# Layer 2's state-space scan laid out as 8 channels x 16 states per tile, and its routing counts in two matmuls

## The reference

```python
xc = silu(conv1d(xi, 4 taps) + conv_b)             # xi, z = split(xn @ W_in), 256 channels each
dt_lo, Bm, Cm = split(xc @ W_xp, [8, 24])          # 8, 16 and 16 columns
delta = softplus(dt_lo @ W_dt + dt_bias)           # 256 channels
def step(h, (dt_t, B_t, C_t, u_t)):                # h: 256 channels x 16 states
    h = h * exp(dt_t[..., None] * A) + (dt_t * u_t)[..., None] * B_t[:, None, :]
    return h, einsum('bdn,bn->bd', h, C_t)
y = (scan(step) + xc * D_skip) * silu(z);  s = y @ W_out + x
# feed-forward: probs = softmax(x @ Wr + br); two best of 16 banks; relu(x W1 + b1) W2 + b2, weighted
```

## Time and profile before

| | |
|---|---|
| median of 3 runs | 4643.89 us (4642.11 to 4647.07) |
| the profiled execution: its time, its span | 4658.04 us, 4656.4 us |
| granted PE clock, mean of the span | 0.793 |
| layer2_route | about 1150 to 1347 us of the span |
| layer2_mix | 1347 to about 2350 us; first scan at 1391.9, last at 2332.0 |

### The profile page before, as it was taken

How to read it: one execution, slowest core, us unless ns; L and a number is a source line. 1 busy time by engine, 2 the same in 40 slices (tenths; PEclk the granted TensorE clock), 3 DMA queues, 4 the chain that set the end, 5 groups by cost and what they waited for, 6 DMA issues and landing times. The chain is left out here.

```text
span 4656.4 us, 50785 instructions
## 1 busy us (share of the span) xinstructions
PE 3423.9 (74%) x17802; PEld 1842.6 (40%) x17802; DVE 2642.8 (57%) x3696; ACT 1828.2 (39%) x3692; POOL 1538.3 (33%) x1231
## 2 busy tenths in 40 slices
PE   5888888883538788788757677676776857778587
PEld 3444444441424344344323334333343334343343
DVE  3444444442547777777655566555665656556565
ACT  3333333331214444444424434344343434434344
POOL 0000000003316665656644253332533424334242
PEclk8888888885557777777768879688797988959789
DMA  1000000002212222222100000000000000000000
GB/s 80 7 7 7 7 7 7 7 5 74 72 42 63 67 67 67 67 67 59 59 16 5 8 1 5 8 5 8 1 5 8 5 8 1 8 6 5 8 1 8
DMA packets 70704, 111.46 MB, mean 24 GB/s; under 512 B 8640, under 2 KB 46016, under 8 KB 69952
## 3 DMA queue, kind: packets, MB, share of 16 engines
q1 hardware_dynamic: 65088, 97.47, 6.5%
q0 software_dynamic: 5376, 11.02, 0.9%
HBM read 81.71 MB, written 26.74 MB: 23 GB/s over the span
## 5 line engine op out<-in xcount | busy, mean ns | idle before, releaser
L369 ACT ACTIVATE l_PT<-PB 128x512 f32<-128x512 f32 x512 | 277.9, 594 | 539.1 <-PE PB L280 539.1
L280 PE MATMUL PB<-l_QM,l_KP 32*128 32x256 f32 x2048 | 375.2, 497 | 131.6 <-DVE l_QM L418 75.9
L407 DVE TENSOR_REDUCE keep_MXP<-PB 128x4 f32<-128x1024 f32 x256 | 301.5, 1220 | 106.8 <-PE PB L253 106.8
L280 PEld LDWEIGHTS PB<-l_QM,l_KP 32*128 32x128 f32 x2048 | 241.3, 243 | 256.4 <-ACT l_PT L369 99.9
L1308 DVE TENSOR_TENSOR_SCAN l_ST<-l_DA,l_DB 128x1024 f32<-128x1024 f32 x128 | 313.7, 2451 | 42.0 <-ACT l_DA L1196 32.8
L1355 POOL TENSOR_TENSOR l_CA<-l_ST,l_CN 128x512 f32<-128x512 f32 x128 | 182.6, 1426 | 397.6 <-DVE l_ST L1308 346.0
L703 POOL MEMSET l_KV<- 128x4 f32 x8 | 0.8, 105 | 918.5 <-POOLq L109 918.5
L1515 POOL TENSOR_TENSOR l_PT<-l_PT,l_PEN 128x512 f32<-128x512 f32 x168 | 212.5, 1284 | 184.5 <-ACT l_PT L369 184.5
L1089 PE MATMUL PB<-l_CA,consts 128*128 128x512 f32 x256 | 199.2, 872 | 71.4 <-POOL l_CA L1355 71.4
L1779 POOL TENSOR_TENSOR l3f_SQ<-l3f_RW 128x512 f32<-128x512 f32 x128 | 146.8, 1147 | 302.4 <-ACT l3f_RW L1645 302.4
L1302 DVE TENSOR_TENSOR l_DB<-l_DU,PB 128x1024 f32<-128x1024 f32 x128 | 155.4, 1214 | 154.1 <-PE PB L1079 153.4
(11 more groups left out here) (416 smaller groups left out, 7934.3 us busy)
## 6 DMA issues: line engine op xcount, KB each, us to landing
l_WB<-in_w2f_dram SPq DMA_DIRECT2D x80, 578.0 KB, 3.4
l_XR<-xs_mid SPq DMA_DIRECT2D x80, 64.0 KB, 3.5
ys_mid<-l_YO SPq DMA_DIRECT2D x80, 64.0 KB, 3.3
w3fs<-in_w3f_dram SPq DMA_DIRECT2D x1, 3125.0 KB, 16.6
keep_XI<-in_x_dram SPq DMA_DIRECT2D x9, 256.0 KB, 3.0
x_mid<-keep_X SPq DMA_DIRECT2D x9, 256.0 KB, 3.0
s_mid<-keep_S SPq DMA_DIRECT2D x9, 256.0 KB, 2.0
keep_SI<-s_mid SPq DMA_DIRECT2D x9, 256.0 KB, 2.6
```

The costliest lines, as they stand in the source:

```text
L280: last = nc.tensor.matmul(PB[:, 4 + u % STBANKS, kt * SEQ:(kt + 1) * SEQ], b.KP[rows, a, i, k0:k0 + 128], b.QM[rows, n % 2, :], start=True ...
L369: nc.scalar.activation(b.PT[:, u % PSLOTS].rearrange("p k q -> p (k q)"), PB[:, 4 + u % STBANKS, :], ACT.Exp).then_inc(s.exp_done, 1)
L407: nc.vector.tensor_reduce(dst[:, 2 * pair:2 * pair + 2, :, 16 + n % 2], PB[:, 2 * pair:2 * pair + 2, :].rearrange("p r (t k) -> p r t k", ...
```

## The change

In the mix, a turn now handles 16 channels instead of one state: partition p of a tile is channel p // 16 of a group of 8 and state p % 16, and the tile has two such groups of 512 tokens. There are still 16 turns a chunk (`PAIRS`).

- B and C depend on the state and the token alone: they are spread once per chunk (head steps 12 and 13, two matmuls with `statesel`, copied by ACT to `BT` and `CT`). `CN` goes.
- delta and delta*x must now be spread from 8 channels to 128 partitions in every turn: `spread_pairs` issues four matmuls of K = 32 (`rowsel`), two from `DL` for the next turn into banks 0 and 1, two from `DU` for this turn into banks 2 and 3. For one turn they lie in the four row strips of the array. ACT `decay` reads banks 0 and 1, DVE `drive` banks 2 and 3.
- POOL multiplies ST by C in place, one instruction of 2 x 512; PE sums over states with ones matrices of 32 columns (`add_states`, four matmuls in the four column strips every second turn, bank 4). Sums are taken by DVE (`take_sums`) twice a chunk.
- The head uses one bank (7) instead of two, one matmul at a time. ACT takes over the copies of xi and z and the bias add of delta; z goes through a copy and one silu of 1024 columns; x_proj is two matmuls instead of four. POOL takes over DU = delta*x (`drives`, turn 13).
- The expert tile uses bank 5 for rows, hidden and the final projection, 6 for out; tiles run in turns 5 to 14 (`FIRST` = 5).
- ST gets four buffers instead of two. Three constants are added (696 columns).
- In the routing stage `counts` is two matmuls of 64 columns, ahead of `ln_tensor` on PE; `place` makes the running base with four small adds and stands behind `ln_vector` on DVE.

```diff
 # layer2_route
-                    for t in range(TT):
-                        o = PB[:, 6, t * E2:(t + 1) * E2]
-                        nc.tensor.matmul(o, c.before, b.OC[:, t, :], start=True, stop=t == 0)
-                        for u in range(t):
-                            nc.tensor.matmul(o, c.ones, b.OC[:, u, :], start=False, stop=u == t - 1)
...
+                    nc.tensor.matmul(PB[:, 6, 0:TT * E2], c.before, each, start=True, stop=True)
+                    nc.tensor.matmul(PB[:, 6, TT * E2:2 * TT * E2], c.ones, each, start=True, stop=True).then_inc(s.count_ready, 1)
...
 # layer2_mix, PE
+                def spread(bank, src, k, n, e):
+                    h, i, strip = place(n)          # n // 8, n % 8 // 2, 2 * (n % 2)
+                    q = 32 * (strip + e)
+                    return nc.tensor.matmul(PB[:, bank + e, :], c.rowsel[q:q + 32, i * 128:(i + 1) * 128],
+                                            src[q:q + 32, k % 2, h, :], start=True, stop=True)
+
+                def spread_pairs(k, n):
+                    g = PAIRS * k + n
+                    ahead = g + 1 < PAIRS * CHUNKS
+                    k1, n1 = divmod(g + 1, PAIRS)
+                    if ahead:
+                        pe.wait_ge(s.decay_ready, g + 1)
+                        if n1 == 0:
+                            pe.wait_ge(s.delta_ready, k1 + 1)
...
+                    if g:
+                        pe.wait_ge(s.drive_done, g)
+                    for e in range(2):
+                        if ahead:
+                            spread(0, b.DL, k1, n1, e).then_inc(s.delta_spread, 1)
+                        spread(PAIR0, b.DU, k, n, e).then_inc(s.drive_spread, 1)
...
+                def add_states(k, q):
+                    h, i, _ = place(2 * q)
+                    pe.wait_ge(s.part_ready, PAIRS * k + 2 * q + 2)
...
+                    for n in (2 * q, 2 * q + 1):
+                        for e in range(2):
+                            strip = 2 * (n % 2) + e
+                            last = nc.tensor.matmul(PB[32 * strip:32 * strip + 32, SUMS, :], c.states[:, 24 - 8 * i:56 - 8 * i], b.ST[:, (PAIRS * k + n) % RING, e, :],
+                                                    start=i == 0, stop=i == 3, tile_position=(0, 32 * strip))
...
 # layer2_mix, ACT
+                    for e in range(2):
+                        act.wait_ge(s.delta_spread, 2 * g + e + 1)
+                        group = 16 * h + 4 * (strip + e) + i
+                        last = nc.scalar.activation(b.DA[:, g % 2, e, :].rearrange("p (s t) -> p s t", t=SEQ)[:, :, 1:SEQ],
+                                                    PB[:, e, :].rearrange("p (s t) -> p s t", t=SEQ)[:, :, 1:SEQ],
+                                                    ACT.Exp, scale=c.aneg[:, group:group + 1])
                     last.then_inc(s.decay_ready, 1)
-                    act.wait_ge(s.c_ready, g + 1)
...
-                    nc.scalar.activation(b.CN[:, g % 2, :], PB[:, 1, :], ACT.Copy).then_inc(s.c_copied, 1)
...
 # layer2_mix, DVE
+                    dve.wait_ge(s.drive_spread, 2 * g + 2)
+                    nc.vector.tensor_tensor(b.DB[:, g % 2], PB[:, PAIR0:PAIR0 + 2, :], b.BT[:, k % 2, :].unsqueeze(1).broadcast_to([128, 2, T]),
+                                            ALU.mult).then_inc(s.drive_done, 1)
...
 # layer2_mix, POOL
+                        nc.gpsimd.tensor_tensor(b.ST[:, g % RING], b.ST[:, g % RING], b.CT[:, k % 2, :].unsqueeze(1).broadcast_to([128, 2, T]),
+                                                ALU.mult).then_inc(s.part_ready, 1)
+                        if n == 13 and k + 1 < CHUNKS:
+                            drives(k + 1)
```

More of the change, by code:

```diff
@@ L56 @@
           ("dist", 2 * SEQ), ("qcos", SEQ), ("qsin", SEQ), ("kcos", SEQ), ("ksin", SEQ), ("rot", 128),
[L57 removed]
+          ("window", 4 * 128), ("expert", E2), ("states", 56), ("statesel", 128), ("rowsel", 512), ("tile", TILES), ("full", TOKENS // 128), ("eps", 1), ("one", 1), ("aeps", 1), ("pow", 1), ("lnnorm", 1)]
 W0 = [("q", NA * 128), ("k", NA * 128), ("v", 128), ("out", NA * 128), ("w2", 1024), ("win", 128), ("w1c", 8),
@@ L1057, in head @@
                     elif step == 9:
-                        pe.wait_ge(s.silu_z, 2 * k + 2)
+                        pe.wait_ge(s.z_copied, 2 * k + 2)
                         pe.wait_ge(s.silu_x, 2 * k + 2)
                         for h in range(2):
-                            nc.tensor.matmul(PB[0:DTR, 6, :], w.xp[:, h * 72:h * 72 + DTR], b.XC[:, p, h, :], start=h == 0, stop=h == 1)
-                        for h in range(2):
-                            last = nc.tensor.matmul(PB[0:64, 7, :], w.xp[:, h * 72 + DTR:h * 72 + 72], b.XC[:, p, h, :], start=h == 0, stop=h == 1)
+                            last = nc.tensor.matmul(PB[0:96, LANE, :], w.xp[:, h * 96:(h + 1) * 96], b.XC[:, p, h, :], start=h == 0, stop=h == 1)
@@ L1092, in project @@
                 def project(k):
                     pe.wait_ge(s.y_gated, k + 1)
-                    pe.wait_ge(s.rows_taken, SLOTS * (k + 1))
+                    pe.wait_ge(s.hid_done, 4 * SLOTS * (k + 1))
                     for h in range(2):
-                        last = nc.tensor.matmul(PB[:, 2, :], w.out[:, h * 128:(h + 1) * 128], b.YG[:, h, :], start=h == 0, stop=h == 1)
+                        last = nc.tensor.matmul(PB[:, WORK, :], w.out[:, h * 128:(h + 1) * 128], b.YG[:, h, :], start=h == 0, stop=h == 1)
@@ L1107, in tile_hidden @@
+                    if j % SLOTS == 0 and k:
+                        pe.wait_ge(s.s_added, k)
+                    nc.tensor.transpose(PB[:, WORK, 0:128], b.XR[:, j % 2, :], c.ident).then_inc(s.rows_ready, 1)
                 def tile_hidden(j):
@@ L1193, in decay @@
+                def decay(k, n):
+                    g = PAIRS * k + n
+                    h, i, strip = place(n)
                     if g >= 2:
                         act.wait_ge(s.state_ready, g - 1)
-                    for h in range(2):
-                        last = nc.scalar.activation(b.DA[:, g % 2, h, :].rearrange("p (s t) -> p s t", t=SEQ)[:, :, 1:SEQ],
-                                                    b.DL[:, p, h, :].rearrange("p (s t) -> p s t", t=SEQ)[:, :, 1:SEQ],
-                                                    ACT.Exp, scale=c.aneg[:, h * NS + n:h * NS + n + 1])
+                    for e in range(2):
+                        act.wait_ge(s.delta_spread, 2 * g + e + 1)
[3 more added lines that the diff above has]
+                                                    ACT.Exp, scale=c.aneg[:, group:group + 1])
```

365 lines of the change are left out of this document (182 added, 183 removed).

## The result

The changed kernel takes 4759.33 us in the median of 4 runs (4755.87 to 4785.53), the kernel before 4645.48 beside it: 1.0252 times as long, 95% interval 1.0209 to 1.0294. It is slower, by 114 us; the forecast was 4869, the range 4680 to 4980. The profiled execution took 4755.87 us with a span of 4754.3, which is 97.9 more than the span before.

What follows compares the result with a forecast made beforehand. No engine was full; expert turns were bound by the weights' load loop (6.97 us), at the low clock by PE itself. Mix +247, last chunk +11, ends +7, routing -40: +225 on 4643.9 gives 4869 us, range 4680 to 4980.

Steps and rivals of the forecast that it cites:

- The loop: Mix, expert turns: the spread waits for ACT's decay behind relus and head; bare loop 6.27 us full clock, 9.41 low.
- the two bounds: Mix: each turn's time at full and at low clock; a chunk 121 or 169 us, against 119.7 before.
- The spreads: Mix, PE: four row strips overlap, 1.05 us a turn at full clock, 2.01 low; twice the spreading costs nothing more.
- The clock: Mix: mostly low clock because PE idles before the decay; a chunk 155 us, +35.3 each, +247 for seven.
- The last chunk: Mix, last chunk without head: 113 us to the last scan, between 96 and 122, against 102.3 before: +11.
- Ends and routing: Ends of the mix, first head, constants, last product: +7; routing stage without the 9.71 us wait for counts: -40.
- The sum: Whole kernel: 247 + 11 + 7 - 40 = +225 us on the median 4643.9, giving 4869, 4.8% slower.
- The clock stays high: Mix rival: four strips keep the array full and PE's clock falls less often; -30 us, 4614; chance 13%.
- The port was the bound: Mix rival: the port shared by DVE and POOL set the pace, a turn gains 1.3 us; 4439; chance 8%.
- The low clock throughout: Mix rival: every turn of the mix runs at the low clock; +330 us, 4974; chance 13%.
- no overlap of the strips: Mix rival: a spread takes two rounds, +1.05 or +2.01 us a turn, about 190 more; 5060; chance 4%.
- What would show it: Signs in the mix: PE busy under 70%, clock about 0.6, chunk near 155 us, turns 7, 11, 12 longest, POOL about 2.7.

Runs made afterwards that it cites:

- the POOL experiment: Kernel before with POOL's second product and its sum cut from 512 to 8 columns in turns 1 to 15: 4597.61 us, 0.9934.
- the decay early: Changed kernel with the next turn's decay moved on ACT ahead of the YO copy, relus and head: 4546.63 us (0.9807), again 4570.99 (0.9819).

## Why the prediction was right, and where it was off

**The loop.** Right. Of the waits before L1094, the spread, the decay ends 240 of 251 (matmuls and weight loads together), and the wait by itself, in the old layout, costs 129 us of mix. The turns, from spread to spread, mean of seven chunks in the first trace of the changed kernel, beside the two bounds of the prediction's table:

| turn | full, low clock (forecast) | measured |
|---|---|---|
| 5, 13 | 7.8, 12.7 | 10.0, 11.8 |
| 6, 10 | 7.0, 10.8 | 7.4, 6.8 |
| 7 | 11.1, 14.2 | 12.4 |
| 8, 14 | 7.0, 9.4 | 8.7, 7.7 |
| 9 | 8.7, 14.7 | 12.5 |
| 11 | 11.0, 15.9 | 12.7 |
| 12 | 10.5, 13.6 | 12.5 |
| sum of the ten | 84.9, 124.2 | 102.5 |
| the six others | 36.2, 44.9 | 38.0 |

Nine of the ten lie between their bounds, and turn 10 is 0.2 us under. Turns 2 and 3 are 15.8 together (16 or 17 forecast).

**The spreads.** Right. Four strips run side by side: instructions start within 0.02 us of each other at 1690.68, and the next matmul can start 1.07 after the first spread (1667.81 to 1668.88; 1.05 taken) or 2.03 at the low clock (1702.27 to 1704.30; 2.01 taken). The prediction's estimate of a spread 0.3 us longer did not come, but the fault is in the estimate: it set the factor of 3.07 against the time of the four strips themselves, not against that of single matmuls. In the kernel before, a full matmul of 512 columns is followed by the next 0.86 us later (this one by the row at 1783.83 in the earlier trace rows):

```profile
1782.97 1.02 PE L1089 MATMUL PB<-l_CA,consts 128*128 128x512 f32 x2
```

Four of these in a row would take 3.44 us, so 1.07 us for four strips is 3.2 times. The Trainium skill (TensorE: Matmul & The Clock Gate, Part 3: Packing small matmuls) gives 3.07 times, and the trace roughly agrees. Going from two strips to four cost nothing: the second instruction of a strip starts 0.53 us after the first in both kernels (1785.64 to 1786.17 and 1667.81 to 1668.34).

**The clock: the term that was mis-sized.** The direction, the loop and the range held; the size was twice what came (+225 forecast, +114 measured), and 102 of the 127 us between the forecast and the difference of the spans are this step. The step "two thirds of the way from 121 to 169 and a little more, 155" measured 140.4, and with it +247 became +145.3 (983.06 - 837.75). I expected a clock near 0.6 and it was 0.71. At 0.71 the low level holds 58% of the time, since 1 - 0.58 x 0.5 = 0.71, and with the two bounds a chunk is then 1 / (0.58/169 + 0.42/121) = 145 us. So 10 of the 14.6 us a chunk lie in the clock, 70 us in all, and the rest in turns that are 3% shorter than my sums. What I had read from the earlier trace rows, low for 23 us on end though PE was busy, was taken as the pattern; but in the changed kernel the clock comes back inside a turn, as at 1706.85, after 4.6 us of work. No row that I had shown had such a return in it.

**The last chunk.** Forecast 113 between 96 and 122, measured 96.2 (2443.7 - 2347.5), before 102.3: -6 instead of +11. Its clock was 0.79; the formula above, with 42% low, gives 105.5, so here half of the miss is the clock and half the sum of the turns.

**Ends and routing.** The ends, +7 forecast, are +5.2 (95.2 - 90.0). The routing stage, -40 forecast, is -35.7 in its stretch, and a chunk 18.43 (18.5 forecast): the wait of 9.71 was the last one.

**The sum.** 225 forecast. The differences are -101.7 for seven chunks, -17.1 for the last, -1.8 for the ends, +4.3 for the routing, and -10.8 for the first and the last part, which the change hardly touches (+3.0 and -13.8, within what they vary by from trace to trace): 97.9, the difference of the two spans.

**The rivals.** *The clock stays high* was false (0.71), though its price for the mix was nearly right: with the gaps filled, clock 0.91, the mix is 942.2, that of the kernel before 940.1. *The port was the bound* fell with the POOL experiment, 30 us instead of 150; but it was right that this layout could gain once the decay runs ahead. With the decay early the mix takes 856 to 879 us against 907 to 940 in the old layout. Which part of the layout gives those 30 to 80 us was not taken apart. *The low clock throughout* and *no overlap of the strips* are excluded by the rows above.

**What would show it.** Busy PE under 70%: 69%. Turns 7, 11 and 12 the longest: yes, with turn 9 beside them. POOL's 2.7 us a turn: 2.52 (282.41 / 112). Clock 0.6 and chunk 155: no, 0.71 and 140.4.

## What to carry to other kernels

When a small instruction of an engine frees a bank that another engine wants at the start of its next turn, place it ahead of the work that itself waits for that other engine; here moving two exponentials forward in ACT's list turned a kernel 2.5% slower than before into one 1.8 to 1.9% faster. Before judging a new layout, put its new wait alone into the old kernel: one line showed that most of the loss was the wait's and not the layout's. For a loop with both clock levels write down the time at each level and treat the share between them as the uncertain number; and for an edit worth under 1%, compare its own stretch in the traces, since other stages move more than that.

## What the hardware showed that was not expected

- The clock came back from 0.50 to 1.00 during 4.6 us of matmuls (1702.27 to 1706.85) and had fallen again after a wait of 2.39 us, where the earlier trace rows have it low for 23 us on end. 1200 matmuls of 384 columns that nothing reads took the clock of the mix from 0.71 to 0.91 and 137 us off its time.
- The same chunk of layer 3 took 280.2, 283.2, 286.7, 289.8, 293.2, 297.1, 300.2 or 303.6 us in the fourteen traces and rarely a value between: steps of 3.0 to 3.9 us, with the clock from 0.86 down to 0.76. In the two traces of the changed kernel the part after the last scan differs by 18 us, of which seven such chunks make 9.
- The mix of the kernel before varies in the same way: in the kernel before with new routing, chunks of 111.7 and 122.4 us stand side by side in one trace (scans at 1589.9, 1701.6 and 1824.0).
- Only what lies in different strips overlaps. In the decay-early version the head's dt matmul reads rows 64 to 95, as one of the four spreads behind it does. The dt matmul and the three other spreads start from 1869.17 to 1869.20, the spread of the same strip at 1870.14, and the ten instructions end at 1871.15, 1.98 us after the first; the eight of four spreads alone take 1.14 (1667.81 to 1668.95).
- An activation table load took 1.28 us and the activation behind it started 0.01 us after its end (1696.12 + 1.28, then 1697.41). The Trainium skill (ScalarE: Activation LUTs, What ACT_TABLE_LOAD costs) adds some 1.4 us of draining for every switch; no such gap is seen here.
